# A graph network's edge layer computed early and kept in memory

## The reference

```python
hid = jax.nn.silu(edge_length_embedded @ fc_w0 / np.sqrt(NB))   # (edges, 8) @ (8, 64)
w = hid @ fc_w1 / np.sqrt(RN)                                   # (edges, 64) @ (64, 256)
wA, wB, wC, wD = (w[:, :MUL], w[:, MUL:2 * MUL], w[:, 2 * MUL:3 * MUL], w[:, 3 * MUL:])
# midA..midD: products of wA..wD with gathered node rows and edge_attr, then
y0 = jax.ops.segment_sum(mid0, edge_dst, num_segments=Nn) * inv_nb
```

## Time and profile before

| | us |
|---|---|
| median of 3 runs | 3844.33 |
| profiled execution, its span | 3966.1 |
| setup | 0 to 41 |
| count matrix stage | 41 to 316 |
| gated graph steps | 470 to 2090 |
| edge loop | 2646 to 3350 |
| PE busy over the span | 3642.8 (92%) |

### The profile page before, as it was taken

How to read it: one execution, slowest core, us unless ns; L and a number is a source line. 1 busy time by engine, 2 the same in 40 slices (tenths; PEclk the granted TensorE clock), 3 DMA queues, 4 the chain that set the end, 5 groups by cost and what they waited for, 6 DMA issues and landing times. The chain is left out here.

```text
span 3966.1 us, 60201 instructions
## 1 busy us (share of the span) xinstructions
PE 3642.8 (92%) x18935; PEld 3087.8 (78%) x18935; DVE 2451.9 (62%) x4843; ACT 1491.9 (38%) x3475; POOL 665.9 (17%) x658
## 2 busy tenths in 40 slices
PE   5999899999999999999996999988888888869996
PEld 2555699999999998999994888657777777848885
DVE  7886655555555555556554666556666665677775
ACT  0363311211211111112114544457777775136663
POOL 0002000000000000000002200025555553012221
PEclk9999999999999999999997999989999999879998
DMA  1353022222222222222222210112222222431113
GB/s 53 65 105 65 26 87 89 65 89 84 70 84 74 80 88 71 83 83 71 83 69 98 72 31 30 42 47 83 81 84 79 84 80 59 150 71 38 38 38 119
DMA packets 265216, 288.48 MB, mean 73 GB/s; under 512 B 70331, under 2 KB 237327, under 8 KB 264283
## 3 DMA queue, kind: packets, MB, share of 16 engines
q1 hardware_dynamic: 233701, 208.44, 18.1%
q0 software_dynamic: 24192, 66.15, 5.8%
q10 hardware_dynamic: 7030, 10.16, 0.7%
HBM read 242.21 MB, written 42.48 MB: 72 GB/s over the span
## 5 line engine op out<-in xcount | busy, mean ns | idle before, releaser
L1043 PE MATMUL bank<-a_wide,parts 125*128 125x448 f32 x4200 | 872.9, 367 | 0.0
L1043 PEld LDWEIGHTS bank<-a_wide,parts 125*128 125x128 f32 x4200 | 785.6, 188 | 78.4 <-issue 9.9
L2288 POOL DMA_INDIRECT rows<-h_dram,src_t x392 | 375.4, 958 | 331.9 <-DVE prod L2483 218.7
L2421 ACT ACTIVATE hot<-eq,ea 128x80 f32<-128x80 f32 x1568 | 405.3, 352 | 1.0 <-DVE eq L2463 0.5
L1093 DVE CAST a_wide<-a_cols 125x2240 fp32r<-125x2240 bf16 x210 | 275.5, 1328 | 138.7 <-PE bank L1043 138.7
L1017 POOL TENSOR_TENSOR nf_g<-nf,nf_g 128x896 fp32r<-128x896 f32 x42 | 95.4, 2271 | 1575.0 <-ACT nf_g L1187 1575.0
L2328 PEld LDWEIGHTS bank<-prod,hot 128*80 128x80 f32 x2352 | 295.9, 153 | 70.9 <-issue 21.6
L2328 PE MATMUL bank<-prod,hot 128*80 128x128 f32 x2352 | 331.8, 277 | 10.6 <-issue 10.4
L1052 PE MATMUL bank<-nf_g,whh 128*128 128x448 f32 x1512 | 339.7, 369 | 0.0
L1052 PE MATMUL bank<-msg,wc 128*128 128x448 f32 x1512 | 339.1, 369 | 0.0
L1052 PEld LDWEIGHTS bank<-msg,wc 128*128 128x128 f32 x1512 | 284.2, 188 | 27.5
(11 more groups left out here) (438 smaller groups left out, 5787.7 us busy)
## 6 DMA issues: line engine op xcount, KB each, us to landing
a_cols<-a_dram SPq DMA_DIRECT2D x210, 546.9 KB
a_dram<-a_cols SPq DMA_DIRECT2D x15, 1250.0 KB, 9.9
w<-in_w SPq DMA_DIRECT2D x4, 2728.0 KB
deg_bc<-deg_dram SPq DMA_DIRECT2D x42, 224.0 KB, 6.0
gate_bc<-gate_dram SPq DMA_DIRECT2D x42, 224.0 KB, 3.2
rows<-h_dram,src_t POOLq DMA_INDIRECT x392
w<-y_rows SPq DMA_DIRECT2D x12, 512.0 KB, 15.1
w<-in_w SPq DMA_DIRECT2D x6, 896.0 KB
```

What stands on the lines that cost most here:

```text
L1043: ins = nc.tensor.matmul(p_msg[f][:, 0:GW], parts[0:SPB, m, c * HB + k, f * 128:(f + 1) * 128], a_wide[u % 2][0:SPB, k, :], start=(c == 0 ...
L2288: nc.gpsimd.indirect_dma_start(out=rows[n % ITC][:, :], out_offset=None, in_=h_dram, in_offset=bass.IndirectOffsetOnAxis(ap=src_t[:, n:n + ...
L2421: ins = nc.scalar.activation(hot[:, q % 2, j, m, :], eq[:, q % 2, j, :], ACT.Copy, scale=ea4[:, q * UC + j, m:m + 1])
```

## The change

The hidden layer leaves the edge loop. In setup ACT and POOL split `ea8` into two parts and ACT's queue stores them (16 rows instead of 24). In the count matrix stage two units at a time (a pair; there are 49) are put into one operand of 128 rows, 32 rows to a unit, and multiplied with a weight matrix that has a block for each unit, so that one matmul 128x512 makes the hidden rows of both. ACT applies Silu and rounds to the high part, POOL subtracts for the low part, and SP stores both (512 KB) to `hid_dram`. Tiles 0 to 7 take three pairs each, tiles 8 to 32 one each. The edge loop loads 128 rows per unit from `hid_dram`, seven units ahead at most. To make room, a set in the count matrix stage has four tiles instead of five.

```diff
-SETS = [5] * 15 + [4]
+SETS = [4] * 19 + [3]
...
 (setup, ACT)
+                act.dma_start(ea[:, :], A["ea8"].rearrange("a (p n) -> (a p) n", p=EP)).then_inc(ea_in, 16)
                 act.dma_start(x_rows[:, :, :], A["x_rows"]).then_inc(x_in, 16)
+                act.wait_ge(ea_in, START + 16)
+                for h, cut in enumerate(ea_cuts):
+                    nc.scalar.activation(ea_parts[0][:, cut], ea[:, cut], ACT.Copy).then_inc(ea_high, 1)
...
 (setup, POOL)
+                    nc.gpsimd.tensor_tensor(ea_parts[1][:, cut], ea[:, cut], ea_parts[0][:, cut], ALU.subtract).then_inc(ea_low, 1)
...
 (adjacency)
+        a = t * HID_AT_ONCE if t < FIRST_HID else FIRST_HID * (HID_AT_ONCE - 1) + t
+        return range(min(a, NIT), min(a + (HID_AT_ONCE if t < FIRST_HID else 1), NIT))
...
 (adjacency, SP)
+                def edges(i):
+                    for u in range(2):
+                        cols = slice((2 * i + u) * UE, (2 * i + u + 1) * UE)
+                        for at, rows in ((0, slice(0, 16)), (16, slice(0, 8))):
+                            r = rows.stop - rows.start
+                            sp.dma_start(ea[i % 2][32 * u + at:32 * u + at + r, :].bitcast(F32), ea8_dram[rows, cols]).then_inc(ea_in[i % 2], 16)
...
+                for n, (start, tiles) in enumerate(sets):
+                    for t in range(start, start + tiles):
+                        for i in pairs_of(t):
+                            if i + 2 < NIT:
+                                sp.wait_ge(hid_mm, START + i + 1)
+                                edges(i + 2)
+                            sp.wait_ge(hid_low, START + i + 1)
+                            sp.dma_start(hid_dram[i].rearrange("m p e -> p m e"), hid[:, i % 2, :, :].bitcast(F32)).then_inc(hid_out[i % 2], 16)
+                    sp.wait_ge(cols_done, START + (start + tiles) * HALVES)
+                    sp.dma_start(a_dram[:, :, start * DW:(start + tiles) * DW], a_cols[n % 2][:, :, 0:tiles * DW]).then_inc(a_stored[n % 2], 16)
...
 (adjacency, POOL)
+                for i in range(NIT):
+                    pool.wait_ge(hid_high, START + i + 1)
+                    nc.gpsimd.tensor_tensor(hid[:, i % 2, 1, :], hid_raw[:, i % 2, :], hid[:, i % 2, 0, :], ALU.subtract).then_inc(hid_low, 1)
...
 (adjacency, PE, behind the rounds of tile t)
+                    for i in pairs_of(t):
+                        pe.wait_ge(fw_step, START + 4)
+                        pe.wait_ge(ea_in[i % 2], START + i // 2 * 64 + 64)
+                        pe.wait_ge(silu_done, START + i - 3)
+                        nc.tensor.matmul(bank[4 + i % 4][:, :], fw[:, :], ea[i % 2][:, :], start=True, stop=True).then_inc(hid_mm, 1)
...
 (adjacency, ACT, behind the eviction of tile t)
+                        for i in pairs_of(t):
+                            act.wait_ge(hid_mm, START + i + 1)
+                            act.wait_ge(hid_low, START + i - 1)
+                            nc.scalar.activation(hid_raw[:, i % 2, :], bank[4 + i % 4][:, :], ACT.Silu, scale=8.0 ** -0.5)\
+                              .then_inc(silu_done, 1)
+                            act.wait_ge(silu_done, START + i + 1)
+                            act.wait_ge(hid_out[i % 2], START + i // 2 * 16)
+                            nc.scalar.activation(hid[:, i % 2, 0, :], hid_raw[:, i % 2, :], ACT.Copy).then_inc(hid_high, 1)
...
 (edge_convolution, SP; hidden, silu and split are gone from PE, ACT and DVE)
-                        sp.dma_start(ea8[0:24, b, :].bitcast(F32), ea8_dram[:, q * UE:(q + 1) * UE]).then_inc(ea_in[b], 16)
+                        sp.wait_ge(w_mm, chunks + max(q - HIDS + 1, 0) * UC)
+                        for m in range(PARTS):
+                            sp.dma_start(hid[m * MUL:(m + 1) * MUL, q % HIDS, :].bitcast(F32),
+                                         hid_dram[pair, m, u * MUL:(u + 1) * MUL, :]).then_inc(hid_in[q % HIDS], 16)
```

More of the change, by code:

```diff
@@ L43 @@
 NIT = NU // 2
+HIDS = 7
+FIRST_HID, HID_AT_ONCE = 8, 3
 UE = UC * EC
@@ L295, in setup @@
         range_i = sb(ctx, "range_i", [NRANGE, 1], I32)
+        ea = sb(ctx, "ea", [128, NCH * EC // EP])
+        ea_parts = [sb(ctx, f"ea_part{m}", [128, NCH * EC // EP], F32R) for m in range(PARTS)]
         with nc.Block() as block:
@@ L841, in adjacency @@
         a_cols = [sb(ctx, f"a_cols{b}", [128, KT, max(SETS) * DW], BF16) for b in range(2)]
+        fw_raw = sb(ctx, "fw_raw", [128, 128])
+        fw_high = sb(ctx, "fw_high", [128, 128], F32R)
+        fw = sb(ctx, "fw", [128, 128], F32R)
+        ea = [sb(ctx, f"ea{b}", [128, UE], F32R) for b in range(2)]
+        hid_raw = sb(ctx, "hid_raw", [128, 2, UE])
+        hid = sb(ctx, "hid", [128, 2, PARTS, UE], F32R)
         def begin(eng, tag):
@@ L944, in _ @@
                         act.reg_alu(rounds, ranges_at[t // AHEAD % 2][t % AHEAD], PACK_BITS, ALU.arith_shift_right)
-                        act.reg_add(turns, turns, rounds)
+                        act.reg_alu(more, rounds, 0, ALU.max)
+                        act.reg_add(turns, turns, more)
                         fetch(act, ranges_at, t + 1)
@@ L1496, in gnn_to_experts @@
         iota_f = sb(ctx, "iota8", [RT, 8])
-        ea = sb(ctx, "ea", [128, NCH * EC // EP])
-        ea_parts = [sb(ctx, f"ea_part{m}", [128, NCH * EC // EP], F32R) for m in range(PARTS)]
         p_back, p_turn, p_hid, p_lg = bank[0:3], bank[3:5], bank[5:7], bank[7]
@@ L2353, in _ @@
                     next_round(pe, regs, per_round)
-                units, chunks, dmas = at_round(pe, regs, per_round)
+                units, chunks, loads = at_round(pe, regs, per_round)
                 pe.wait_ge(added, units)
@@ L2408, in _ @@
                     units, chunks = at_round(act, regs, per_round)
-                    def silu(q):
-                        act.wait_ge(hid_mm, units + q + 1)
-                        act.wait_ge(hid_done, units + q - 1)
-                        nc.scalar.activation(hid_raw[:, q % 2, :], p_hid[:, 0:UE], ACT.Silu, scale=8.0 ** -0.5)\
-                          .then_inc(silu_done, 1)
                     def weighted_hots(q):
@@ L3103, in layouts @@
     pad8[:, :E0] = i["L0_ffn_router_w2"]
+    fw0 = np.zeros((128, 128), np.float32)
+    for u in range(2):
+        fw0[32 * u:32 * u + 24, MUL * u:MUL * u + MUL] = np.tile(np.asarray(i["L1_gnn_fc_w0"]), (3, 1))
     vec = np.concatenate([np.arange(MUL)] + [MUL + 3 * np.arange(MUL) + k for k in range(3)])
```

176 lines of the change are left out of this document (81 added, 95 removed).

## The result

| | before | changed |
|---|---|---|
| median, us | 3844.57 (4 runs) | 3895.37 (4 runs) |
| ratio | 1 | 1.0132 (1.0118 to 1.0147) |
| first round in the count matrix stage | 44.67 | 52.06 |
| first to last round of the stage | 268.2 | 342.2 |
| first to last sums of the edge loop | 694.2 | 546.1 |

The change makes the kernel 51 us slower; 47 were forecast. One number needs a word first: chips differ. The kernel before takes 3844 us on two chips and 3964 us on a third, and the span of its profile (3966.1 us) says that it was most likely profiled on one like the third, while the changed kernel was profiled on one like the first two. The difference lies nearly all in the edge loop.

What follows compares the result with a forecast made beforehand. PE was taken to lead both stages. Count matrix stage +74, setup +4 and -1.3, loop matmul -22.5, loop start -5.5, rest -1.5 gave +47 us: 3844.3 to 3891 us, range 3837 to 3935.

Steps and rivals of the forecast that it cites:

- (b): Count matrix stage, tiles 0 to 7: PE waits 2.7 us for each tile's third load, 21.6 us over 8 tiles.
- (c): Count matrix stage: loads on SP's queue come behind sets' stores; six PE waits of 4 us plus one, 28 us.
- loads pass the stores: Rival, chance 0.22: small loads in the count matrix stage are not held behind stores; total +18, 3862 us.
- (a): Count matrix stage: 49 new matmuls on PE at 0.23 us each, 11.3 us.
- (e): Count matrix stage: about 14 new waits bring PE to half clock; between 0 and 17, taken as 8 us.
- (f): Count matrix stage: POOL's 49 subtractions hold DVE at their shared port, delaying PE; 0 to 13.5, taken as 3 us.
- (d): Count matrix stage: stores of four-tile sets cost as much as those of five; 0 to 5, taken as 2 us.
- Setup: Setup: POOL's subtractions beside DVE and the store of 16 rows add 4 us; the moved table load gives -1.3.
- Edge loop and its start: Edge loop: the hidden matmul goes, 22.5 us saved; a shorter chain to the first sums saves 5.5 us.
- stay as they are: Edge loop: joint pauses, most of the profile's 121.8 us excess over the timed median, assumed unchanged.
- faster: Rival, chance 0.12: PE makes up its waits using DVE's four full slots; stage grows 14 us, total -13, 3831 us.
- The loop gives more: Rival, chance 0.09: losing Silu and splits gives up to 46 us more in the edge loop; 3845 us, no change.

Runs made afterwards that it cites:

- e2: Changed kernel with four operand buffers instead of two, loads issued four pairs ahead instead of two: 3856.66 us, ratio 1.003 to the kernel before.
- e3: Changed kernel with the sets' stores issued on ACT's queue instead of SP's: 3886.85 us, ratio 1.011 to the kernel before.
- e6: Changed kernel with the loads of the seven longest-awaited pairs issued on ACT's queue: 4028.97 us beside 3963.79 for the kernel before, ratio 1.0161.
- e4: Changed kernel with filling matmuls of 400 columns put before PE's waits for loads: 3890.96 us, ratio 1.0114 to the kernel before.
- e5: Changed kernel with POOL's 49 subtractions in the count matrix stage cut to 16 columns: 4037.16 us beside 3963.79 for the kernel before, ratio 1.018.
- e1: Changed kernel without the 49 pairs' work in the count matrix stage, so its result is not the reference's: 3822.66 us, ratio 0.9946 to the kernel before.
- e11: Changed kernel with sets of five tiles, three tables of relative positions instead of four: 3899.2 us, ratio 1.0151 to the kernel before.
- e8: Changed kernel with the low part of setup's split made on DVE instead of POOL: 4041.38 us beside 3963.79 for the kernel before, ratio 1.0192.
- e10: Changed kernel with x_rows loaded in the count matrix stage and setup's POOL subtractions in 16 pieces: 3894.39 us beside 3844.24 for the kernel before, ratio 1.0135.
- e12: Changed kernel run again unaltered as a control: 3896.77 us beside 3844.24 for the kernel before on the same chip, ratio 1.0136.

## Why the prediction was right

By its steps, forecast first:

- **(b) third loads, 21.6.** Seven waits of 2.25 to 3.48 us and the common part of tile 4's, together 21.4. Right, by the trace, though the last of the seven (2.25) ended with ACT's Silu and not with a load. With the loads further ahead (e2) they went.
- **(c) loads behind a set's store, 28.** Six waits at exactly the six tiles named and the rest of tile 4's: 29.6 + 6.0 = 35.6 us, at the upper end that I gave (35). Place and cause of release are right, the reason is mostly not: I put it down to the order of SP's queue and took the store's landing as the price. e3 and e6 show that on another queue three quarters of the waiting remain, and that a load sent behind a store takes its 9 to 10 us on either one. The price came out near because both reasons let the loads land with the store. The rival "loads pass the stores" gave this term 3 us and is wrong.
- **(a) the matmuls, 11.3.** Mis-sized. In tiles without a wait they cost less than nothing: 2.84 us a tile for 3.02. Each new tile began with 0.20 us of PE idle time before; now the matmul stands in that gap. Part of it is catching up, as these tiles come behind a wait: in e2, where they don't, a tile takes 3.13 us, which is 0.11 more than before for the matmul and POOL's effect on DVE together.
- **(e) the clock, 8.** The clock fell as expected, and the rounds' busy time rose by 13.6 us, more than I had. To restore the clock gave 3.1 us of stage (e4), so 8 is neither confirmed nor refuted.
- **(f) the port, 3.** 1.7 (e5), inside the spread. POOL's cost on DVE is real, and covered.
- **(d) sets of four, 2.** Nothing (e1), nor did sets of five help (e11).
- **Setup, 2.7.** 7.4, or 5.8 to 9.1 by the other kernels' first rounds. I counted one cause at a time, with DVE's waits as cover; e8 and e10 point to two causes side by side, each of which may cover the other.
- **Edge loop and its start, -28 and others -1.5.** The profile of the changed kernel gives 5.58 us from unit to unit, where the earlier trace rows's stretch before had 5.86 us: 98 x 0.28 = 27.4, and the start 5.3. Together -33, counted against 51 - 7.4 - 74.0 = -30 of the total.

The stage's sum came out at 74.0 for 74, by errors that cancel: waits 57.9 where (b) and (c) had 49.6, the other terms 16.1 where they had 24.3. The assumption that the pauses "stay as they are" did not hold on the second chip, where the loop gave back next to nothing and the kernels nearest to the changed one cost 73 us (e5) and 78 us (e8). It did no harm on the timed chips because the changed kernel has no pauses there. So the total is near by luck in two places, here and in the stage.

Of the rivals, "faster" rested on PE making up its waits. It did so by little: 0.18 us a tile. One sign that I gave for being wrong, rounds under 1.1 us, is met all the same, and the sign was badly made. The 1.17 us came from tile 0; a tile near number 20 has three rounds (twelve matmuls) in its 3.02 us, so 1.01 a round before any change, and not 2.6 rounds of 1.17. DVE, with 0.95 us a round, had next to nothing to spare there, where I gave it 0.22. "The loop gives more" was wrong on both kinds of chip.

## What to carry to other kernels

Before moving work into a stage that a compute engine leads, read its DMA share by stretch and not as a mean: with a share of 0.40 over the whole stage before the change, small loads issued with or behind a set's store needed 9 to 10 us on either queue, and those issued just ahead of it cost no wait. What helped was to issue early. When a wait is removed, ask what it hid: late loads hid late stores, and over 30 of the stage's 74 us stayed under every arrangement tried. A profile tells which engine leads on the chip where it was taken; compare its span with the timed runs before trusting a gain.

## What the runs showed of the hardware

- Four loads (96 KB in all) on a queue with nothing else took 7.3 us from the last issue to use while a store of 1000 KB in 320-byte pieces ran from another (e6); one load on a free machine took 1.8 us. From the first issue it was 9.2 to 10.1 us on the store's own queue and 9.5 to 10.3 on the other. Issuing four such loads behind the store took up to 7.13 us instead of 1.38 (changed kernel).
- With a matmul of 512 columns at the seam between two tiles' rounds, a tile took 2.84 us instead of 3.02 in the changed kernel, and 3.13 in e2.
- With 260 extra matmuls the granted clock between 130 and 160 us was 1.00 instead of 0.73; the rounds took 11.4 us less over the stage and the stage 3.1 less (e4).
- The same program took 3843 and 3844 us on two chips and 3964 on a third. For the changed kernel the traces put nearly all of such a difference in one loop (e8 and e12).
